# Thirty unread matmuls behind the last projections, and one unread matmul over 112 rows per opening tile in place of two over 48

## The reference, cut to what matters

```python
q = _rope(proj(Wq, bq))
k = _rope(proj(Wk, bk))
v = proj(Wv, bv)
scores = jnp.einsum('bhtd,bhsd->bhts', q, k) / scale
attn = jax.nn.softmax(scores, axis=-1)
out = jnp.einsum('bhts,bhsd->bhtd', attn, v)
```

## Time and profile before

| | |
|---|---|
| median of three runs | 2943.38 us (2934.75 to 2955.72) |
| profiled execution | 2935.19 us |
| its span | 2933.4 us |
| TensorE busy | 2798.8 us (95%) |
| VectorE busy | 2318.3 us (79%) |
| ScalarE busy | 2116.1 us (72%) |
| GpSimd busy | 969.0 us (33%) |
| granted TensorE clock, mean over the span | 0.972 |

### The profile page before, as it was taken

One profiled execution on the slowest core, in us unless ns is written; L12 is line 12 of the kernel. 1 busy time (PEld: TensorE's weight loads), 2 busy tenths in 40 slices (PEclk: granted clock), 3 DMA queues, 4 the chain that ended last, 5 costly groups with the idle time before them and its releaser, 6 DMA issues. The chain is left out here.

```text
span 2933.4 us, 59060 instructions
## 1 busy us (share of the span) xinstructions
PE 2798.8 (95%) x22548; PEld 1746.8 (60%) x22548; DVE 2318.3 (79%) x4282; ACT 2116.1 (72%) x4556; POOL 969.0 (33%) x1147
## 2 busy tenths in 40 slices
PE   7899999999999999999975899999999999999997
PEld 7743333333333333333344688888887788888886
DVE  7779999999999999999624677777776777777774
ACT  5568888888888888888844566666665666666763
POOL 7500000010001000000026455555554556556563
PEclk9869999999999999999987999999999999999999
DMA  5603324443344334433221000000001100000000
GB/s 163 187 18 52 54 42 60 61 74 59 65 69 63 66 59 69 60 58 61 31 82 72 5 4 5 5 4 5 4 5 33 54 12 19 19 15 15 19 18 25
DMA packets 84360, 131.32 MB, mean 45 GB/s; under 512 B 32944, under 2 KB 58992, under 8 KB 76272
## 3 DMA queue, kind: packets, MB, share of 16 engines
q1 hardware_dynamic: 77792, 120.41, 20.9%
q10 hardware_dynamic: 6288, 7.14, 0.8%
HBM read 83.98 MB, written 34.61 MB: 40 GB/s over the span
## 5 line engine op out<-in xcount | busy, mean ns | idle before, releaser
L659 ACT ACTIVATE probs<-scores 128x512 f32<-128x512 f32 x2048 | 1114.5, 596 | 201.0 <-PE scores L588 78.7
L692 DVE TENSOR_REDUCE mx<-aux 128x1 f32<-128x1024 f32 x982 | 1201.1, 1223 | 63.0 <-PE aux L556 55.8
L556 PE MATMUL aux<-k_stack,q_stack 48*128 48x512 f32 x2006 | 759.5, 454 | 5.2 <-DMA k_stack<-qk_dram 3.2
L588 PE MATMUL scores<-q_stack,k_stack 50*128 50x512 f32 x2048 | 763.3, 451 | 0.0
L601 PE MATMUL pv<-probs,v_ones 128*32 128x256 f32 x8192 | 659.9, 394 | 0.1
L588 PEld LDWEIGHTS scores<-q_stack,k_stack 50*128 50x128 f32 x2048 | 311.0, 186 | 430.0 <-ACT probs L659 412.5
L601 PEld LDWEIGHTS pv<-probs,v_ones 128*32 128x32 f32 x8192 | 161.8, 108 | 362.2 <-ACT probs L659 288.0
L556 PEld LDWEIGHTS aux<-k_stack,q_stack 48*128 48x128 f32 x2006 | 307.3, 189 | 37.0 <-DVE mx L692 17.0
L507 POOL CAST m_parts<-head_max 128x16 fp32r<-128x16 f32 x32 | 6.3, 197 | 935.5 <-DVE head_max L685 935.5
L1438 ACT ACTIVATE VO<-VO,wo_bo_sb 128x256 f32<-128x256 f32 (+1 forms) x512 | 250.7, 491 | 47.3 <-DVE wo_bo_sb L1562 47.0
L1333 PE MATMUL bank<-q_minus_first,q_stack 128*128 128x256 f32 x2112 | 268.7, 286 | 0.6 <-DVE x_sb L1593 0.6
(11 more groups left out here) (169 smaller groups left out, 4360.8 us busy)
## 6 DMA issues: line engine op xcount, KB each, us to landing
q_stack<-qk_dram SPq DMA_DIRECT2D x192, 128.0 KB, 5.2
k_stack<-qk_dram SPq DMA_DIRECT2D x192, 128.0 KB, 7.0
qk_dram<-qkT_hi SPq DMA_DIRECT2D x32, 256.0 KB, 3.5
qk_dram<-qkT_lo SPq DMA_DIRECT2D x32, 256.0 KB, 4.0
VO<-o_stage SPq DMA_DIRECT2D x128, 32.0 KB, 6.9
q_minus_first<-sums_dram SPq DMA_DIRECT2D x32, 128.0 KB, 3.0
w_parts<-tables SPq DMA_DIRECT2D x16, 256.0 KB, 2.5
out<-x_sb SPq DMA_DIRECT2D x16, 256.0 KB, 2.8
```

The lines of the kernel that those rows point to most:

```text
L556: return nc.tensor.matmul(out, q_stack[max_rows, n % BODY, tile * P:(tile + 1) * P], k_stack[max_rows, n % BODY, keys * 512:(keys + 1) * 512],
L588: last = nc.tensor.matmul(out, k_stack[0:SCORE_ROWS, n % BODY, s * P:(s + 1) * P], q_stack[0:SCORE_ROWS, n % BODY, j * 512:(j + 1) * 512], ...
L659: nc.scalar.activation(probs[:, e % PROBS], scores[:, item_of_exp(e) % BANKS1], ACT.Exp, scale=float(D1) ** -0.5).then_inc(act_emptied, 1)
L692: nc.vector.tensor_reduce(mx[:, n % BODY, tile, half:half + 1], aux[:, unit % 2].rearrange("p a k -> p (a k)"), AX.X, ALU.max).then_inc(dv ...
```

## The change: what it does

In the projection phase TensorE gets a helper `keep_busy(times)`, which issues so many matmuls of 128 rows by 128 columns of weights and 512 moving columns into a bank of `psT` that is no longer read. It issues 6 of them at step 32 and 6 at step 33, each time ahead of the wait for `rot_done`, and 18 behind the last transposes. In the opening the two unread matmuls of a tile (L616) go, and behind the second difference of each tile one unread matmul over the partitions 0 to 111 of `k_stack` comes in.

```diff
@@ project_phase, block.tensor
+            def keep_busy(times):
+
+                for _ in range(times):
+                    nc.tensor.matmul(psT[:, 0], w_hi[:, 0, 0:P], w_lo[:, 0, 0:512], start=True, stop=True)
+
...
                 if exists(t - 2):
                     v = t - 2
+                    if t >= NT:
+                        keep_busy(6)
                     pe.wait_ge(rot_done, v + 1)
...
                     last.then_inc(qkT_in_psum, 1)
+            keep_busy(18)
@@ attention_phase, first_difference
                 nc.tensor.matmul(out, q_minus_first[rows, t], k_stack[rows, n, k * 512:(k + 1) * 512], start=False, stop=True).then_inc(act_filled, 1)
-                nc.tensor.matmul(pv[:], q_stack[max_rows, n, tile * P:(tile + 1) * P], k_stack[max_rows, n, k * 512:(k + 1) * 512], start=True, stop=True)
+                if k == 1:
+                    nc.tensor.matmul(pv[:], k_stack[0:max_rows.stop, n, 0:P], k_stack[0:max_rows.stop, n, 0:512], start=True, stop=True)
```

## The result

The changed kernel took 2945.55 us in the median of 12 runs (2941.51 to 2964.68), beside 2930.16 us (2928.48 to 2955.72) for the kernel before in 12 runs. The ratio is 1.0047, 95% interval 1.0029 to 1.0065: 0.5% slower, some 14 us (8 to 19). That is less than 1%, as forecast, and on the side that was forecast. The predicted 2947 us was close because two errors met: the added 5 us were too few, and the median of three runs from which I counted lay 13 us above that of twelve. That the time came so near is luck.

The account below looks back on a forecast made before the run. The opening was taken as bound by TensorE at half clock. Terms 0 + 0 - 0.7 + 5.6 gave +5 us, added to the median and rounded down to 2947 us; own range 2937 to 2962, with the first rival 2907 to 2962.

Parts of the forecast that it names:

- The fillers: End of the projections: twelve in TensorE's idle time and eighteen beside SyncE's last stores, each group costing 0 us.
- The fall of the clock: Start of the opening: clock falls within the first two tiles after 2.4 us of nothing; full clock until then saves 0.7 us.
- The wide matmul doesn't bring the clock back: Opening: with one wide slot in five, the clock was taken to stay low.
- The price of the fifth slot: Opening: five slots in place of four at half clock, 0.26 to 0.43 us a tile, 5.6 us taken for 20 tiles.
- Its weights load beside the running matmul, as those of L276 do: Opening: the new 112-row matmul's weight load was taken to be hidden beside the matmul then running.
- the 0.16 of the first slot: Opening: a tile's first slot is 0.59 us, its extra wait put down to VectorE being just behind TensorE.
- The return of the clock: Steps behind the opening: kept where it was; each half step that it returns later costs 0.93 us.
- The base: Whole kernel: the 5 us were added to the median of the runs shown, 8.2 us above the profiled execution.
- The first rival: Clock holds from the projections on, 1.38 us a tile in the opening: 2912 us, 31 us under the median; chance 0.27.

Follow-up runs that it names:

- e1: The kernel before with only the 30 unread matmuls behind the last projections, opening unchanged: 2931.37 us, ratio 0.9988 to before.
- e4: The changed kernel with 28 in place of 18 fillers behind the last transposes: 2928.23 us, ratio 0.9961 to the kernel before.
- e7: The kernel before with 14 unread 112-row matmuls in a row between the opening and the first step: 2935.20 us, ratio 1.0003.
- e11: The kernel before with one unread 48-row matmul a tile over partitions 0 to 47 in place of L616: one execution, 2935.54 us.
- e2: The kernel before with the wide matmul in place of L616 and no fillers: 2956.83 us, ratio 1.0069 to before.
- e3: The kernel before with L616 deleted, so no unread matmul in the opening: 2935.46 us, ratio 1.0004 to before.
- e12: The changed kernel with the old opening, 28 last fillers, unread wide matmuls behind the 19th tile and three groups of four in the first steps: 2929.53 us, ratio 0.9979.
- e8: e6 with the old opening, two unread 48-row matmuls a tile in place of the wide one: 2929.20 us, ratio 0.9987 to before.
- e6: e4 with unread 112-row matmuls around the transposes of the maxima and one with each of the first six scores: 2919.30 us, ratio 0.9953 to before.

## Why the prediction was right, and where it was not

**The fillers: right.** All thirty at no cost, opening at 127.41; e1 confirms it by time.

**The fall of the clock: right.** It was expected in the first two tiles, from the 2.4 us without a matmul; it came in the stretch 128 to 130 after 2.32 us. e4 shows the pause as the cause: with ten more fillers, and 0.48 us in its place, the same opening kept full clock for 32 us.

**The wide matmul doesn't bring the clock back: right.** 0.50 from there to 197. The rule of the Trainium skill (TensorE: Matmul & The Clock Gate, "What's actually happening") that activity releases the throttle needs the kind of activity beside it here: 14 wide matmuls in a row did it in some 3 us in e7, a busy opening of 48-row ones with one wide in five slots did not in 57.

**The price of the fifth slot: the term that was mis-sized.** The prediction took 0.26 to 0.43 us a tile and measured was 0.85; for the 20 tiles it took 5.6 and should have taken 17. Two sentences failed. The first is "Its weights load beside the running matmul, as those of L276 do". An L276 has matmuls over all rows on both sides, and e11 shows that a 48-row matmul among 48-row ones behaves so too (2.13, the lower end of my bound). The wide one stands between 48-row ones. Its load is recorded at 136.43, with the matmul itself, and both of its edges stand open, 0.13 in front and 0.30 behind. The rows that I had read show the same edges. In a half step of before, L601 follows a 48-row slot, and its start comes 0.55 us behind the pair's and not 0.43:

```profile
189.30 0.62 PE L588 MATMUL scores<-q_stack,k_stack 50*128 50x512 f32 x1
...
189.85 1.08 PE L601 MATMUL pv<-probs,v_ones 128*32 128x256 f32 x8
```

The prediction put such a half step down as 0.59 + 0.43 and products, and did not ask what the change of rows costs. The loads recorded late support the weight load as the cause; that it is the load alone, and not something else in the change from part of the rows to nearly all, no run parts.

The second is that the 0.16 of the first slot "came from VectorE being just behind", for which I went to the lower end. In the changed kernel VectorE is 1.49 us idle ahead of each maximum (e2 shows the same opening) and the first slot is still 0.59. In before the wait for VectorE lies ahead of 131.62, in every second tile, and a matmul whose load begins only with it is followed by a slot of 0.59:

```profile
131.62 0.28 PEld L556 LDWEIGHTS aux<-k_stack,q_stack 48*128 48x128 f32 x1 [0.69 <-DVE mx L700]
```

Behind the wide matmul the load of the next L622 comes late as well, so the 0.16 stays with another origin; in e11, where no load is late on those rows, it is gone.

**The return of the clock: not foreseen.** I kept the number of slow half steps. The clock came back at the same point of the span (197) in both profiled executions while the opening ended 15 us later, so 7 fewer half steps were slow, which paid back 6.7 us of the loss in that pair. That is chance rather than a rule: in the profiled executions of e3, e1 and e2, whose openings ran at half clock too, it came back at 202.5, 206.8 and 212.9. The medians lie 15 us apart, near the 17 of the tiles, with little paid back.

**The base.** The three runs had a median of 2943.38, the twelve one of 2930.16, and on the chips of the experiments 35 runs of before one of 2937.55 and 29 one of 2934.84. I had put the spread down to the return of the clock behind the opening. That is part of it; e1 and e12 show another, a late load of `k_stack` deep in the steps, behind which the clock is at half for 44 and 51 us, worth some 20 us.

**The first rival** fell for the reason held against it, the pause, but its price was wrong too: a tile at full clock takes 1.53 (e8) to 1.56 us (e4) and not 1.38, since the ring of two units, or with the wide matmul its open edges, bind before VectorE does. So an opening at full clock is worth 20 x (1.87 - 1.56) = 6 us and not 10.

## What to carry to other kernels

Unread matmuls hold a clock only if they reach to the work behind them: here the fall came behind a pause of 2.32 us and not behind one of 0.48. Count the time from the last filler to the next matmul, and from there on every wait in the thin stretch behind. Where the clock stays low, a wide unread matmul is dear, since between matmuls on part of the rows it costs two slots (0.85 us); put several in a row. A slot on the rows that its neighbours use is cheap (0.26), but no run here shows that it does anything for the clock. And judge a change of half a percent by twelve runs, not by three, where some executions lose the clock by chance, and compare versions that ran on different chips by their ratios to the kernel before, not by their medians.

## What the runs showed that I had not expected

- The same opening, with two unread 48-row matmuls a tile, keeps full clock if it starts with it (e8: 1.00 from 128 to 162, TensorE busy 26.45 of 34 us) and does not regain it if it starts without (before: 0.50, TensorE busy 40.98 of 41.60 us).
- The first steps lose the clock easily: at 180.4 in e7, at 165.1 in e6 and e12, at 163.1 in e8. No product with the values had been made by then, but for the first few in e7 (179.80).
- A wide matmul between 48-row ones at full clock costs 0.52 us, its own 0.43 and the 0.09 by which L624's slot of 0.32 in front of it is longer than 0.23 (134.75, 135.07, 135.50 in e4), against 0.23 in a row of its like.
